# VectorE's order in the second half of an attention-and-MLP pass: the reciprocal behind the first two maxima, the normalisation behind the sixth, the first gate behind the seventh

## The chip, the core and the metric

The kernel runs on one core of one Trainium2 chip. Its time is the device time of one execution in microseconds (us), lower is better; the number that counts is the median of several executions. The core has TensorE (PE in the rows, its weight loads PEld), VectorE (DVE), ScalarE (ACT), GpSimd (POOL) and SyncE (SP, which here only issues DMAs). Each engine works through its own list of instructions in the order in which the program gives them, and waits for the others by semaphores.

## What is computed

The input is 16 sequences of 256 tokens with 288 channels, and a conditioning vector for each. A rotation comes first (a 64-dimensional subspace of the channels is rotated by a matrix exponential made from the conditioning), and then three transformer layers of the same form, of which this is the core:

```
ada = silu(c) @ W_ada + b_ada              # six rows of 288: shifts, scales, gates
h = modulate(layernorm(x), shift_a, scale_a)
q, k, v = split(h @ W_qkv + b_qkv)         # 16 heads of 18
attn = softmax(q @ k.T * 18 ** -0.5)       # over 256 keys
x = x + gate_a * ((attn @ v) @ W_proj + b_proj)
h = modulate(layernorm(x), shift_f, scale_f)
x = x + gate_f * (gelu(h @ W_fc1 + b_fc1) @ W_fc2 + b_fc2)
```

## The kernel before

**Stages.** `prepare` computes the rotation and the conditioning rows; the rest, about nine tenths of the time, is `layers`. There one *pass* works on one sequence of one layer; 3 layers of 16 sequences are 48 passes, numbered `it = l * B + b`. Matrix products are done with a value split in a high and a low part (`split`), so that most operands exist twice: the high part is written by ScalarE, and GpSimd subtracts it from the full value (`low`) for the low part.

**A pass is a software pipeline over three sequences.** `half_step(l, b)` is written once for each engine, and each engine's version says what that engine does in pass `it`: the softmax and weighted values of sequence `it`, the output projection and MLP of `it - 1`, and the queries, keys, scores and maxima of `it + 1` (the norm of `it + 2` too). `whole_run` calls `prologue`, then the passes (the ones with b from 2 to 13 in a loop, b = 0, 1, 14 and 15 written out, since weights are converted in them), then `epilogue`. Nothing but the written order and the semaphores decides what stands behind what.

**TensorE's second half of a pass** (`half_step` of the tensor block): `up(m, 0)` to `up(m, 4)` are the first MLP product of the sequence before, with `score_units(it + 1, 0)` ahead of `up(m, 3)`. Then come `attention_transposes(it + 2)`, `score_units(it + 1, 2)`, `down(m, 0, 0)`, `down(m, 0, 1)`, `score_units(it + 1, 4)`, `down(m, 0, 2)`, `down(m, 1, 0)`, `score_units(it + 1, 6)`, `down(m, 1, 1)`, `down(m, 1, 2)`. A call of `score_units(it, u)` makes the raw scores of the head pairs u and u + 1 in the two PSUM tiles `scores0` and `scores1` (L1840); from u = 2 on it waits until VectorE has read both tiles (`s_max`). The next pass begins with `projection(it, 0)` (L1754 with `w_out`, `o_att`), which waits for both halves of `o_att`'s low part (`s_o_lo`) and for the first gate (`s_down_gated`), then `maxima_transposes`, `projection(it, 1)`, `qk_tiles`, and later `mlp_transposes` (L1770), which waits for VectorE's second `qk_low` and for `x_hat`.

**VectorE's second half of a pass**: `inverse(it)` takes the reciprocal of the softmax sums (L2093; 128 x 32 elements that arrive by a DMA, `s_sum`). `unit_max(it + 1, u)`, eight times, reduces the scores of one head pair to maxima (L2088). `normalise(it)` multiplies the attention output `o_full` by the inverse sums in two halves (L2100), once these have been spread over partitions by four DMAs (`s_inv_ld`). `gate_down(it - 1, t)` multiplies the second MLP product by its gate (L2136), for the two halves t of the tokens; it frees the PSUM tile that the projection of the next pass writes. The next pass begins with `gate_projection` (L2108), `mlp_norm` (L2026, L2031), `qk_low` (L2064) and `x_hats` (L2041).

**ScalarE** issues the DMAs around the sums from its own queue, between its other work: `gather_sums` (L1628), `load_sums` (L1633), and then, between the five `gelu` calls (L1661, L1662), `store_inverse` (L1642, waits for the reciprocal) behind `gelu(2)`, and `spread_inverse` (L1648) behind `gelu(3)` and `gelu(4)`. Behind them come `high_o` (L1638, the high part of `o_att`, waits for `normalise`) and the six evictions of `attention_modulate(it + 2)` (L1574).

**GpSimd** does the low parts. Its list around the end of a pass is

```
for half in range(2): low(o_att[1][:, half, :], ...)   # s_o_lo, L1395
add_mlp(it - 1, 0)        # x_out, waits for gate_down(it - 1, 0), L1523
attention_low(it + 2)     # h_att, two instructions, L1395
add_mlp(it - 1, 1)        # x_out, waits for gate_down(it - 1, 1)
# next pass
add_attention(it)         # x_one, two halves, L1486: waits for gate_projection
inverse_deviation(1, it)  # the norm's rstd, L1390, L1392
```

VectorE's `mlp_norm` waits for `x_one`, its `x_hats` for `rstd`.

Of the kernel before, what the change touches and what calls it, by code (L numbers as in the profile page):

```python
# [998 lines left out]
def layers(nc, dram, keep):  # L999
# [3 lines left out]
    with ExitStack() as ctx:  # L1003
# [262 lines left out]
        def neighbours(l, b):  # L1266

            start = isinstance(l, int) and isinstance(b, int) and l == 0 and b == 0
            final = isinstance(l, int) and isinstance(b, int) and l == L - 1
            return not start, not (final and b >= B - 1), not (final and b >= B - 2)  # L1270
# [741 lines left out]
        def _(dve):  # L2012
# [20 lines left out]
            def x_hats(order, it, x_tile, done):  # L2033
                dve.wait_ge(s_var[order], 2 * it + 2)
                dve.wait_ge(s_rstd[order], it + 1)
                for t in range(2):

                    for out, part in ((x_hat[:, t, 0:C], x_tile[:, t, :]),
                                      (x_hat[:, t, C:MOD_WIDTH].rearrange("p (n c) -> p n c", n=2),
                                       x_tile[:, t, 2 * P:C].unsqueeze(1).to_broadcast([P, 2, C - 2 * P]))):  # L2040
                        nc.vector.tensor_scalar(out, part, mean_var[:, t, 0:1], rstd[:, 1, t:t + 1],  # L2041
                                                ALU.subtract, ALU.mult).then_inc(done, 1)
# [16 lines left out]
            def qk_low(it, n):  # L2059
                dve.wait_ge(s_qk_hi, QK_USES * it + n + 1)  # L2060
                tiles = slice(2 * n, min(2 * n + 2, QK_TILES))
                rows = qk_rows_of(2 * n)
                width = (tiles.stop - tiles.start) * T
                tt(qk[1][0:rows, tiles, :].rearrange("p a t -> p (a t)"), qk_bank[n][0:rows, 0:width],  # L2064
                   qk[0][0:rows, tiles, :].rearrange("p a t -> p (a t)").bitcast(F32), ALU.subtract)\
                    .then_inc(s_qk_lo, 1)
# [24 lines left out]
            def inverse(it):  # L2091
                dve.wait_ge(s_sum, 16 * it + 16)
                nc.vector.reciprocal(inv_few[:, :], sums[:, :]).then_inc(s_inv, 1)  # L2093
# [8 lines left out]
            def gate_projection(it):  # L2102
                dve.wait_ge(s_gate_a, 16 * it + 16)
                for t in range(2):
                    dve.wait_ge(s_proj, 2 * it + t + 1 + PRE)

                    dve.wait_ge(s_x_out, 2 * it - 1 + t + PRE2)
                    tt(gated[:, t, :], token_bank[t][:, 0:C], gate_a[:, :], ALU.mult).then_inc(s_proj_gated, 1)  # L2108

            def mlp_norm(it):  # L2110
                norm(1, it, x_one, lambda t: dve.wait_ge(s_x_one, 2 * it + t + 1 + PRE), s_xhat_m)
# [35 lines left out]
            def half_step(l, b):  # L2147
                it = l * B + b
                before, after, after_next = neighbours(l, b)
                if before:  # L2150
                    gate_projection(it - 1)
                    mlp_norm(it - 1)
                if after:
                    qk_low(it + 1, 0)
                if before:

                    dve.wait_ge(s_tr_a, TRS * (it + 2 if after else it + 1))
                    x_hats(1, it - 1, x_one, s_xhat_m)
                if after:
                    qk_low(it + 1, 1)  # L2160
                    qk_low(it + 1, 2)
                if before:
                    mlp_modulate(it - 1, it + 2 if after else it + 1)
                    mlp_high(it - 1)
                if after_next:
                    attention_norm(it + 2)
                if after_next:

                    dve.wait_ge(s_tr_a, TRS * (it + 2))
                    dve.wait_ge(s_tr_m, TRS * it + PRE)  # L2170
                    x_hats(0, it + 2, x_in, s_xhat_a)
                if at(b, 1):
                    convert_weights(l, OF["w_down"], "down")
                if at(b, B - 2) and after_next:

                    dve.wait_ge(s_qk_ps, QK_USES * (it + 2))
                    convert_weights(l + 1, OF["w_in"], "qk")
                if at(b, B - 1) and after:

                    dve.wait_ge(s_v_ps, 2 * it + 2 + PRE)  # L2180
                    convert_weights(l + 1, OF["w_in"], "v")
                inverse(it)
                if at(b, 1):
                    convert_weights(l, OF["b_down"], "down")
                for u in range(8):
                    if u == 4:
                        normalise(it)
                    if u == 6 and before:
                        gate_down(it - 1, 0)
                    if after:  # L2190
                        unit_max(it + 1, u)
                if before:
                    gate_down(it - 1, 1)
# [135 lines left out]
```

## Time and profile before

| | us |
|---|---|
| median of 3 runs (lowest, highest) | 2189.09 (2180.36, 2191.14) |
| the profiled execution, its own time | 2181.43 |
| span of the instructions in it | 2179.7 |
| TensorE busy (share of the span) | 1946.7 (89%) |
| VectorE busy | 1202.7 (55%) |
| ScalarE busy | 1172.5 (54%) |
| GpSimd busy | 1163.0 (53%) |

A pass lasts some 39 us. The profile has one line for each engine and group of instructions, a list of waits (who was idle until whom) and a timeline of one stretch. All times inside the program are counted from the start of the span. In the timeline a line merges neighbours of one kind: start, length, engine, line of the program, what is written from what, count, and in brackets the idle time before it with the instruction that ended it. The letters PEclk stand for the clock that TensorE was granted, as a share of full speed. The passage that the prediction follows is pass 19 (layer 1, b = 3), which begins its second half at 1006 us and whose reciprocal starts at 1012.99.

### The profile page before, as it was taken

What the parts mean: (1) busy time and instruction counts of PE and PEld (TensorE: products, weight loads), DVE (VectorE), ACT (ScalarE), POOL (GpSimd) and SP (SyncE); (2) the same over time, 40 slices, a digit from 0 to 9 for tenths busy, and PEclk for the clock granted to TensorE, in tenths of its full rate; (3) what the DMA queues carried; (4) which work ended last, traced back from release to release, by engine and by line L of the source; (5) the groups of instructions that cost most, each with busy time, mean ns of one, the idle gap of its engine ahead of it and who ended that gap; (6) DMA issues with size and microseconds to landing.
All of it is one profiled execution on the core that took longest, in us unless ns stands there. A gap on an engine that the chain in (4) does not pass through costs nothing. (4 is left out here: it accounts for less than half of the span.)

```text
span 2179.7 us, 51741 instructions
## 1 busy us (share of the span) xinstructions
PE 1946.7 (89%) x17367; PEld 1652.0 (76%) x17367; DVE 1202.7 (55%) x2735; ACT 1172.5 (54%) x2026; POOL 1163.0 (53%) x1511
## 2 busy tenths in 40 slices
PE   5785689999999898889999999999799999999987
PEld 2554578888888787678888888787678888888876
DVE  6883555455455575555465464574565455554641
ACT  3333455656556555555656556555555556555553
POOL 1003555655555555755655655656655656555543
PEclk9896799999999999999999999999999999999998
DMA  6432433323323333433323323233323323333220
GB/s 181 118 119 86 145 94 87 98 75 101 94 68 106 86 86 97 145 93 83 101 76 94 101 81 100 79 89 108 123 76 92 101 70 106 85 90 94 75 77 25
DMA packets 113198, 207.41 MB, mean 95 GB/s; under 512 B 46213, under 2 KB 62723, under 8 KB 112047
## 3 DMA queue, kind: packets, MB, share of 16 engines
q1 hardware_dynamic: 62766, 127.30, 20.8%
q0 software_dynamic: 25296, 49.71, 8.0%
q10 hardware_dynamic: 25040, 29.18, 4.8%
q8 instruction: 53, 0.87, 0.2%
q14 instruction: 43, 0.34, 0.0%
HBM read 99.51 MB, written 20.82 MB: 55 GB/s over the span
## 5 line engine op out<-in xcount | busy, mean ns | idle before, releaser
L2088 DVE TENSOR_REDUCE maxima<-scores 128x4 f32<-128x1024 f32 x384 | 449.5, 1213 | 91.0 <-PE scores L1840 90.9
L1903 PE MATMUL mlp_ps<-h_mlp,w_up 128*128 128x256 f32 (+1 forms) x3024 | 421.8, 291 | 29.6 <-ACT hidden L1662 26.0
L1903 PEld LDWEIGHTS mlp_ps<-h_mlp,w_up 128*128 128x128 f32 (+1 forms) x3024 | 377.3, 191 | 72.3 <-ACT hidden L1662 34.6
L1614 ACT ACTIVATE probs<-scores 128x1024 f32<-128x1024 f32 x384 | 372.4, 1023 | 82.7 <-PE scores L1864 79.4
L1754 PE MATMUL mlp_ps<-w_down,hidden 128*128 128x288 f32 x2592 | 395.5, 306 | 0.0
L1754 PEld LDWEIGHTS mlp_ps<-w_down,hidden 128*128 128x128 f32 x2592 | 365.6, 195 | 12.2
L1395 POOL TENSOR_TENSOR hidden<-g_full,hidden 128x512 fp32r<-128x512 f32 (+1 forms) x240 | 278.9, 1174 | 153.6 <-ACT hidden L1662 152.6
L1283 POOL DMA_DIRECT2D k_stack<-qk x576 | 295.5, 528 | 30.1 <-issue 18.8
L2093 DVE RECIPROCAL inv_few<-sums 128x32 f32<-128x32 f32 x48 | 16.9, 353 | 452.9 <-DMA sums<-sum_scratch 452.9
L1840 PE MATMUL scores<-k_stack,q_stack 54*128 54x256 f32 x1536 | 149.0, 315 | 95.4 <-DVE maxima L2088 73.1
L1661 ACT ACTIVATE g_full<-mlp_ps 128x512 f32<-128x512 f32 (+1 forms) x240 | 133.3, 555 | 162.1 <-issue 56.4
L1395 POOL TENSOR_TENSOR o_att<-o_full,o_att 128x512 fp32r<-128x512 f32 x96 | 121.8, 1290 | 173.5 <-ACT o_att L1638 173.5
L1840 PEld LDWEIGHTS scores<-k_stack,q_stack 54*128 54x128 f32 x1536 | 109.0, 195 | 134.4 <-DVE maxima L2088 82.7
L1395 POOL TENSOR_TENSOR h_mlp<-h_full,h_mlp 128x512 fp32r<-128x512 f32 x48 | 72.3, 1507 | 246.4 <-DVE h_mlp L2054 246.2
L1878 PE MATMUL pv_ps<-probs,v_sb 128*32 128x256 f32 x3072 | 200.9, 391 | 0.8 <-ACT probs L1614 0.8
L1754 PE MATMUL mlp_ps<-w_out,o_att 128*128 128x288 f32 x1152 | 172.7, 300 | 1.7 <-issue 1.7
L1754 PEld LDWEIGHTS mlp_ps<-w_out,o_att 128*128 128x128 f32 x1152 | 158.9, 191 | 3.1 <-issue 2.1
L1864 PE MATMUL scores<-q_stack,k_stack 55*128 55x256 f32 x1536 | 146.1, 310 | 4.5 <-ACT probs L1614 3.1
L1604 ACT ACTIVATE neg_max<-att_ps 16x256 fp32r<-16x256 f32 x48 | 18.0, 374 | 234.5 <-PE att_ps L1850 234.5
L1864 PEld LDWEIGHTS scores<-q_stack,k_stack 55*128 55x128 f32 x1536 | 106.4, 190 | 49.2 <-ACT probs L1614 29.5
L1811 PE MATMUL att_ps<-h_att,w_in 128*108 128x256 f32 (+3 forms) x1008 | 137.4, 284 | 5.8 <-POOL h_att L1395 5.1
L1878 PEld LDWEIGHTS pv_ps<-probs,v_sb 128*32 128x32 f32 x3072 | 86.0, 111 | 67.0 <-issue 12.9
(230 smaller groups left out, 2921.1 us busy)
## 6 DMA issues: line engine op xcount, KB each, us to landing
q_stack<-qk SPq DMA_DIRECT2D x288, 90.0 KB
k_stack<-qk POOLq DMA_DIRECT2D x288, 90.0 KB, 3.2
inv_sum<-inv_scratch ACTq DMA_DIRECT2D x192, 128.0 KB, 2.6
k_stack<-qk POOLq DMA_DIRECT2D x288, 54.0 KB, 3.5
x_mid<-out_x SPq DMA_DIRECT2D x48, 288.0 KB, 4.2
out_x<-x_out SPq DMA_DIRECT2D x48, 288.0 KB, 3.1
x_in<-out_x SPq DMA_DIRECT2D x47, 288.0 KB, 4.0
q_stack<-qk SPq DMA_DIRECT2D x144, 54.0 KB
```

The source lines that it names most:

```text
L1283: engine.dma_start(stack[first:first + HD, units, :].bitcast(F32), qk[part][row:row + HD, src, :].bitcast(F32)).then_inc(signal, 16)
L1395: tt(out, full, high.bitcast(F32), ALU.subtract).then_inc(signal, 1)
L1604: evict(neg_max[:, :], att_ps[0:H, 0:T], ACT.Copy, scale=-1.0).then_inc(s_neg, 1)
L1614: evict(probs[:, u % 4, :, :, :], scores[u % 2][:, :, :, :], ACT.Exp, scale=SCALE)\
L1661: evict(g_full[:, n % 2, 0:width], bank[:, 0:width], ACT.Gelu_apprx_tanh).then_inc(s_gelu, 1)
L1754: last = mm(out, a(left), c(weights[w]), start=start and n == 0, stop=stop and n == total - 1)
L1811: last = mm(qk_bank[n][0:cols.stop - cols.start, (m % 2) * T:(m % 2 + 1) * T], w[:, cols], h, start=count == 0, stop=count == 6)
L1840: last = mm(scores[v % 2][:, par, qt, :], q_stack[r, v, qt * P:(qt + 1) * P], k_stack[r, v, :], start=True, stop=True, tile_position=(R * ...
L1864: last = mm(scores[v % 2][:, par, kt, :], k_stack[r, v, kt * P:(kt + 1) * P], q_stack[r, v, :], start=True, stop=True, tile_position=(R * ...
L1878: last = mm(pv_ps[32 * i:32 * i + 32, (g % 2) * T:(g % 2 + 1) * T], v_sb[:, kt, 4 * g + i, :], probs[:, u % 4, i % 2, kt, :], start=kt == ...
L1903: last = mm(up_bank[n % 2][:, (m % 2) * T:(m % 2 + 1) * T], w[:, m * P:(m + 1) * P], h, start=count == 0, stop=count == 6)
L2088: nc.vector.tensor_reduce(out=maxima[:, :, :, u].rearrange("p q r -> p r q"), in_=scores[u % 2][:, :, :, :], axis=AX.X, op=ALU.max).then_i ...
```

## The change

The three steps `inverse`, `normalise` and the first `gate_down` are called at other places between the eight `unit_max`. Nothing else is touched: the instructions, their waits and the lists of all other engines stay as they were.

```diff
-                inverse(it)
                 if at(b, 1):
                     convert_weights(l, OF["b_down"], "down")
                 for u in range(8):
-                    if u == 4:
+
+                    if u == 2:
+                        inverse(it)
+                    if u == 6:
                         normalise(it)
-                    if u == 6 and before:
+                    if u == 7 and before:
                         gate_down(it - 1, 0)
                     if after:
                         unit_max(it + 1, u)
```

VectorE in the looped passes, first around the reciprocal (L2093), behind the `x_hat` of the sequence two ahead. In the list `x2`, `x4` count merged instructions; ISA rows are waits, REGISTER_ALU rows compute the value waited for.

```order
 L2041 TENSOR_SCALAR x_hat<-x_in,mean_var,rstd 128x64
+L2084 ISA
+L2088 TENSOR_REDUCE maxima<-scores 128x2x2
+L2084 REGISTER_ALU
+L2088 TENSOR_REDUCE maxima<-scores 128x2x2
 L2092 ISA
 L2093 RECIPROCAL inv_few<-sums 128x32
-L2084 ISA
+L2084 REGISTER_ALU
 L2088 TENSOR_REDUCE maxima<-scores 128x2x2
```

The first two maxima now stand ahead of the reciprocal and of its wait for the sums (L2092).

VectorE, same passes, the end of the list up to the second gate, before:

```order
866 L2096 ISA
867 L2100 TENSOR_TENSOR o_full<-o_full,inv_sum 128x512 x2
868 L2084 REGISTER_ALU
869 L2088 TENSOR_REDUCE maxima<-scores 128x2x2
870 L2084 REGISTER_ALU
871 L2088 TENSOR_REDUCE maxima<-scores 128x2x2
872 L2136 TENSOR_TENSOR gated<-mlp_ps,gate_f 128x288
873 L2084 REGISTER_ALU
874 L2088 TENSOR_REDUCE maxima<-scores 128x2x2
875 L2084 REGISTER_ALU
876 L2088 TENSOR_REDUCE maxima<-scores 128x2x2
877 L2136 TENSOR_TENSOR gated<-mlp_ps,gate_f 128x288
```

and in the changed kernel:

```order
867 L2084 REGISTER_ALU
868 L2088 TENSOR_REDUCE maxima<-scores 128x2x2
869 L2084 REGISTER_ALU
870 L2088 TENSOR_REDUCE maxima<-scores 128x2x2
871 L2096 ISA
872 L2100 TENSOR_TENSOR o_full<-o_full,inv_sum 128x512 x2
873 L2084 REGISTER_ALU
874 L2088 TENSOR_REDUCE maxima<-scores 128x2x2
875 L2136 TENSOR_TENSOR gated<-mlp_ps,gate_f 128x288
876 L2084 REGISTER_ALU
877 L2088 TENSOR_REDUCE maxima<-scores 128x2x2
878 L2136 TENSOR_TENSOR gated<-mlp_ps,gate_f 128x288
```

The fifth and sixth maxima have moved ahead of the normalisation (L2100) and its wait (L2096), and one more maximum stands ahead of the first gate (L2136).

## Rows read from the trace of the kernel before

**Rows 1.** The page, part 1: busy time, share of the span, instructions.

```profile
PE 1946.7 (89%) x17367; PEld 1652.0 (76%) x17367; DVE 1202.7 (55%) x2735; ACT 1172.5 (54%) x2026; POOL 1163.0 (53%) x1511
```

**Rows 2.** The waits: who for whom, us in total, times, longest.

```profile
DVE inv_few L2093 <- DMA sums<-sum_scratch: 452.9, 48, 14.3
...
PE scores L1840 <- DVE maxima L2088: 73.1, 47, 5.2
```

**Rows 3.** Timeline of TensorE, 1009 to 1036 us (pass 19).

```profile
1010.30 0.73 PE L1840 MATMUL scores<-k_stack,q_stack 54*128 54x256 f32 x8 [0.56 <-DMA k_stack<-qk]
...
1014.01 0.38 PE L1770 MATMUL pv_ps<-ident,x_hat 128*96 128x128 f32 x2
1015.61 0.74 PE L1840 MATMUL scores<-k_stack,q_stack 54*128 54x256 f32 x8 [1.22 <-DVE maxima L2088]
1016.52 0.40 PE L1912 MATMUL mlp_ps<-b_down,ones_l 128*128 128x288 f32 x1 [0.18 <-ACT hidden L1662]
...
1019.23 0.74 PE L1840 MATMUL scores<-k_stack,q_stack 54*128 54x256 f32 x8
...
1025.77 1.75 PE L1754 MATMUL mlp_ps<-w_out,o_att 128*128 128x288 f32 x12
```

**Rows 4.** Timeline of VectorE, 960 to 1060 us (pass 19's part).

```profile
1012.99 0.35 DVE L2093 RECIPROCAL inv_few<-sums 128x32 f32<-128x32 f32 x1 [9.74 <-DMA sums<-sum_scratch]
...
1016.16 2.36 DVE L2088 TENSOR_REDUCE maxima<-scores 128x4 f32<-128x1024 f32 x2 [0.61 <-PE scores L1840]
1018.85 1.30 DVE L2100 TENSOR_TENSOR o_full<-o_full,inv_sum 128x512 f32<-128x512 f32 x2 [0.33 <-DMA inv_sum<-inv_scratch]
1020.06 2.35 DVE L2088 TENSOR_REDUCE maxima<-scores 128x4 f32<-128x1024 f32 x2
1022.32 0.45 DVE L2136 TENSOR_TENSOR gated<-mlp_ps,gate_f 128x288 f32<-128x288 f32 x1
...
1030.75 0.46 DVE L2026 BATCH_NORM_STATS2 stats<-x_one 128x6 f32<-128x288 f32 x1 [0.56 <-POOL x_one L1486]
```

**Rows 5.** Timeline of all engines, 1006 to 1060 us: ScalarE's.

```profile
1019.57 1.24 ACT L1638 ACTIVATE o_att<-o_full 128x512 fp32r<-128x512 f32 x2 [1.40 <-DVE o_full L2100]
...
1022.96 0.56 ACT L1574 ACTIVATE h_att<-pv_ps,mods 96x256 fp32r<-96x256 f32 x1
```

**Rows 6.** The same timeline, GpSimd's.

```profile
1020.28 2.54 POOL L1395 TENSOR_TENSOR o_att<-o_full,o_att 128x512 fp32r<-128x512 f32 x2 [3.00 <-ACT o_att L1638]
...
1022.93 0.80 POOL L1523 TENSOR_TENSOR x_out<-x_one,gated 128x288 f32<-128x288 f32 x1
...
1023.68 2.10 POOL L1395 TENSOR_TENSOR h_att<-h_full,h_att 128x512 fp32r<-128x512 f32 x2
...
1026.51 0.80 POOL L1523 TENSOR_TENSOR x_out<-x_one,gated 128x288 f32<-128x288 f32 x1 [0.73 <-DVE gated L2136]
...
1029.90 0.81 POOL L1486 TENSOR_TENSOR x_one<-x_mid,gated 128x288 f32<-128x288 f32 x1 [0.92 <-DVE gated L2108]
```

**Rows 7.** Timeline of TensorE's weight loads, 1009 to 1036 us.

```profile
1034.97 0.63 PEld L1770 LDWEIGHTS mlp_ps<-ident,x_hat 128*128 128x128 f32 x6 [0.19 <-DVE qk L2064]
```

**Rows 8.** Timeline of TensorE, 835 to 846 us (pass 15, b = 15).

```profile
838.92 0.74 PE L1840 MATMUL scores<-k_stack,q_stack 54*128 54x256 f32 x8
...
843.62 0.40 PE L1912 MATMUL mlp_ps<-b_down,ones_l 128*128 128x288 f32 x1
```

**Rows 9.** Timeline of VectorE, 836 to 843 us (pass 15).

```profile
839.14 0.35 DVE L2093 RECIPROCAL inv_few<-sums 128x32 f32<-128x32 f32 x1 [12.85 <-DMA sums<-sum_scratch]
```

**Rows 10.** Timeline of all engines, 930 to 938 us (pass 17, b = 1).

```profile
931.64 0.35 DVE L2093 RECIPROCAL inv_few<-sums 128x32 f32<-128x32 f32 x1 [7.37 <-DMA sums<-sum_scratch]
...
936.83 0.40 PE L1912 MATMUL mlp_ps<-b_down,ones_l 128*128 128x288 f32 x1
```

**Rows 11.** Windows, reciprocal to reciprocal, of passes 19 and 6: length, busy times, PEclk, DMA share, GB/s.

```profile
1012.99:1051.65 38.66, 37.27 (x337) 32.09 (x336) 21.38 (x40) 23.01 (x38) 22.54 (x31) 1.00 0.34 92
473.03:513.33 40.30, 38.42 (x336) 33.33 (x335) 21.47 (x41) 23.01 (x38) 22.64 (x31) 0.96 0.32 88
```

## The prediction, made before the changed kernel ran

> **What bounds the kernel now.** I read the page first [rows 1]: TensorE is busy for 89% of the span, every other engine for about half of it. So only what makes TensorE wait, or takes a wait from it, changes the time. The waits come second [rows 2]: the longest of all, 452.9 us in 48 passes, is VectorE's for the sums ahead of the reciprocal, and it costs VectorE nothing it needs; the one that the change is about is TensorE's for the maxima, 73.1 us in 47 waits. Third, the timeline of one pass. In pass 19 TensorE is through with the transposes of `x_hat` at 1014.01 + 0.38 = 1014.39, waits 1.22 us for the first two maxima, makes the scores from 1015.61 to 1016.35, waits once more, 0.18 us, for ScalarE's last gelu, and begins the second MLP product at 1016.52 [rows 3]. The maxima are late because VectorE has them behind the reciprocal, whose sums land only at 1012.99 [rows 4], although their scores were begun at 1010.30 [rows 3]. In 36 of the 39 passes with b from 2 to 14 these distances are the same (the second scores start 2.61 to 2.62 us behind the reciprocal). From 1016.52 on TensorE has no gap above 0.2 us up to 1035; `mlp_transposes` at 1034.97 then wait 0.19 us for VectorE [rows 7]. That is the bound in one sentence: sums, reciprocal, the rest of the gelus, and from there TensorE itself, with its neighbours just in time.
>
> **The change, part by part**, in pass 19 and against its own clock times.
>
> *Two maxima ahead of the reciprocal.* The first maximum of a pair starts 1016.16 - 1015.61 = 0.55 us behind the start of its scores, and two take 2.36 us [rows 3, 4]. With scores at 1010.30 they run from 1010.85 to 1013.21, and the reciprocal, which overlaps the last one by some 0.08 us, starts at 1013.13 instead of 1012.99. It is late where the scores lead it by less than 2.83 us. Over the 39 passes the lead is 2.3 to 3.7 us with a median of 3.05; in those that fall short the shortfalls add up to 1.6 us in all, which I take as the price.
>
> *What TensorE gets.* Its second scores can start at 1014.39 instead of 1015.61, so the wait of 1.22 us goes. What is late next is ScalarE: store of the reciprocal, `gelu(3)`, the first two spreading DMAs and `gelu(4)` stand in one queue behind the reciprocal, and the second MLP product starts 1016.52 - 1012.99 = 3.53 us behind it, today with 0.18 us of wait for that gelu [rows 3, 4]. The reciprocal comes no earlier, so the product starts at 1016.52 as before, only that TensorE now waits 1.4 us ahead of it in one piece. Gain: 0. The third and fourth maxima get earlier, and nobody waits for them: the next scores stand behind 18 products and start at 1019.23 either way [rows 3].
>
> Here a rule of the Trainium skill speaks the other way. Its page "Perfetto Trace Analysis", section "Optimization Strategy", says to look for the gaps of the engine that bounds the kernel, find the semaphore behind each, and make that dependency come sooner, which is what this edit does. By it alone the time would fall by all of the 73.1 us; by the row of the next wait it falls by nothing. The rule is silent on a second wait right behind the first.
>
> *The normalisation behind the sixth maximum.* Today it starts at 1018.85, as soon as its DMAs land [rows 4]. In the new order it stands behind the maxima 5 and 6, whose scores start at 1019.23 [rows 3]: first maximum at 1019.23 + 0.55 = 1019.78, and the instruction behind a pair starts 1022.32 - 1020.06 = 2.26 us after the pair [rows 4], so 1022.04. That is 3.19 us later. Behind it hang, with their durations unchanged: ScalarE's high parts (1019.57), GpSimd's low parts (from 1020.28 for 2.54 us, end 1022.82, that is 3.97 us behind the normalisation's start) and ScalarE's six evictions for the sequence after next (end 1023.52) [rows 4 to 6]. The low parts now end at 1022.04 + 3.97 = 1026.01. The projection waits for them, and starts today at 1025.77 [rows 3]: it had 2.95 us to spare and is asked for 3.19. With about 0.1 us for the semaphore (an estimate, from the 0.05 to 0.2 us between end and start in these rows) it starts 0.35 us late. In return the seventh and eighth scores no longer wait for a VectorE held up by the normalisation (some 0.1 us), which the wait for the low parts swallows.
>
> *What is queued behind on GpSimd.* This is the larger term. Today GpSimd has room after the low parts: `x_out` 1022.93, `h_att` from 1023.68 for 2.10 us, then a gap of 0.73 us, `x_out` 1026.51, a gap, `x_one`, a gap of 0.92 us, `x_one` from 1029.90 to 1030.71 [rows 6]. Shifted, the same list runs without a gap: first `x_out` 1026.12, `h_att` 0.75 us later at 1026.87 (ScalarE's evictions end at 1023.52 + 3.19 = 1026.71, just in time), end 1028.97, second `x_out` 1029.07, then the two `x_one` at 0.75 us each, 1029.82 and 1030.57, end 1030.57 + 0.81 = 1031.38. That is 0.67 us later than 1030.71. VectorE's statistics start 0.04 us behind this end today [rows 4]; on them hang `rstd`, `x_hat` and, in VectorE's list behind `x_hat`, the second `qk_low`, for which TensorE's transposes wait [rows 7]. So TensorE, already 0.35 us late, waits 0.3 us more there and is 0.67 us late in all. Nothing behind it takes this back: TensorE is the bound from there to the weighted values, and the sums of the next reciprocal hang on those. So a pass becomes 0.67 us longer.
>
> *The first gate behind the seventh maximum.* VectorE's list: normalisation 1022.04 to 1023.34, seventh maximum, gate at about 1024.4, end 1024.85, eighth maximum, second gate at 1025.97 as today. The first gate moves by about 2.1 us; its readers are the projection, which now starts at 1026.1, and the first `x_out`, at 1026.12. Cost 0; without the late low parts it would have had 0.9 us to spare. SP's queue gets its next gate load and store behind other waits of the next pass: 0.
>
> *The passes written out.* b = 15, two times with a successor: scores come late there, at 838.92, so the reciprocal moves from 839.14 to 838.92 + 2.83 = 841.75; the product starts 3.53 us behind it, at 845.3, today at 843.62 [rows 8, 9]: +1.65 each, with the 0.67 together +4.6. b = 1, three times: today the conversion of `b_down` stands between reciprocal and maxima, and the product starts at 936.83; with the maxima made earlier it starts 3.53 us behind the reciprocal, 931.64 + 3.53 = 935.17 [rows 10]. I take -1.66 twice and -0.8 in the first layer, with the 0.67 -2.1. b = 0: there the normalisation waits long for its DMAs and holds back maxima 5 and 6; that goes, but GpSimd's queue then sets the pace: -0.5 each, between 0 and -2.4. Pass 0: +0.9. Pass 46 lacks `h_att` on GpSimd: +0.35.
>
> **The sum**: 38 x 0.67 = 25.5; reciprocals 1.6; 4.6 - 2.1 - 1.0 + 0.9 + 0.35 = 2.8; together +29.9 us. Against the profiled execution's own time, 2181.4, this is 2211. The median of the three runs lies 7.7 us above that execution and the lowest below it, so I add half of the distance: **2215 us**. Bounds of the one unknown, the handover: 0.05 us instead of 0.1 makes 0.6 a pass (+27), a further 0.2 us somewhere in GpSimd's list, which has no gap left, 0.87 (+37).
>
> **Rivals.**
> *Faster.* The wait for the maxima was the true limit and the gelus would come in time, or 1.4 us in one piece is worth more than two waits. It decides at the start of the second product: only if it comes earlier than 3.53 us behind the reciprocal. The most it can give is 73.1 us (2181 - 73 = 2108). Against it stands the 0.18 us that TensorE waits there for ScalarE today [rows 3]. 4%.
> *No change.* The normalisation had slack, as the 2.95 us say, and `x_one` is taken in time because GpSimd's list runs closer than its rows. Then only the written-out passes and the reciprocals count, 1.6 + 1.0: 2184 to 2192. It decides whether `x_one` ends later than 1030.71 on pass 19's clock. 10%.
> *Slower through the clock.* Pass 6 is 40.30 us long, pass 19 38.66; in pass 6 the granted clock averages 0.96, in 19 it is 1.00 [rows 11]: that is some 3 us (0.04 x 40.30 / 0.5) at the lower of the two levels, 1.2 instead of 2.4 GHz, and they follow the idle time ahead of the second product. In 8 of the 39 passes this happens, for about 1.5 us each. The new order joins the idle pieces and adds two short ones; if every pass fell, 30 x 1.5 = 45 us would be added: 2260. The idle sum ahead of the product is the same (1.4 us), so I expect the number of such passes to stay near 8, within 5: 7.5 us either way. The Trainium skill ("TensorE: Matmul & The Clock Gate", section "HAM oscillation — how this bites in real kernels") tells of kernels that fall back to the lower level at each wait; here most passes wait and do not fall. 6% for a fall in most passes.
>
> **How the numbers follow.** The forecast, with its mechanism and 20 to 45 us more, has 80%. The range reaches from 2200 (0.45 us a pass against the profiled execution) to 2236 (0.87 a pass, against the highest run, and a few more slow stretches). 0.5%, 11 us, is what a measurement of this kernel can tell from no change. Faster by more than that 5%, within it 10%, slower 85%.
>
> **What the profile of the changed kernel would show.** TensorE's wait for L2088 nearly gone, and in its place one of about 1.4 us a pass for ScalarE's `hidden` ahead of L1912. The product 3.53 us behind the reciprocal, as now. The normalisation 2.8 us behind the start of the third pair of scores. A new wait of TensorE for GpSimd's `o_att` ahead of the projection, about 0.3 to 0.5 us, and one of about as much for VectorE's `qk` ahead of L1770. GpSimd without a gap from `o_att` to the second `x_one`. Passes of 39.3 us instead of 38.7. The prediction is wrong if the product starts earlier behind the reciprocal, if the projection waits for nobody and `x_one` ends no later against it, or if the slow stretches of the clock change by more than five.

## The result, and the profile after

| | before | after |
|---|---|---|
| median, us (lowest to highest) | 2185.86 (2180.36 to 2191.14) | 2224.24 (2220.32 to 2230.86) |
| ratio, 95% interval | | 1.0179 (1.0141 to 1.0217) |
| span of the profiled execution, us | 2179.7 | 2223.3 |
| granted clock of TensorE over the span | 0.956 | 0.945 |
| second MLP product behind the reciprocal, us | 3.52 | 3.51 |
| normalisation behind the reciprocal | 5.99 | 9.05 |
| GpSimd's low parts of `o_att` end behind it | 9.97 | 13.01 |
| projection starts behind it | 12.78 | 13.15 |
| second `x_one` ends behind it | 17.73 | 18.44 |
| `mlp_transposes` start behind it | 21.98 | 22.49 |
| projection to projection, undisturbed passes | 38.81 | 39.26 |

Slower, as forecast, and inside the range. The rows from the third on are medians over the passes with b = 3 to 13 in which TensorE's clock did not fall and GpSimd's DMA issue was not held up: 24 passes before, 19 after ("undisturbed passes" below; the six places in a pass, each as its distance from the reciprocal, are called landmarks).

The page of the changed kernel, parts 1 and 2:

```profile
PE 1973.9 (89%) x17367; PEld 1673.3 (75%) x17367; DVE 1201.9 (54%) x2735; ACT 1171.9 (53%) x2026; POOL 1159.8 (52%) x1511
...
PEclk9896799999999998999999999998999999999998
```

Against [rows 1], TensorE is busy 27 us longer with the same 17367 products. Nothing was added to its work, so some of it ran slower; this is the first sign of the part that the prediction had at zero. The waits (who for whom, us in total, times, longest):

```profile
PE mlp_ps L1912 <- ACT hidden L1662: 72.6, 43, 3.1
...
PE mlp_ps L1754 <- POOL o_att L1395: 14.9, 41, 6.2
...
PE scores L1840 <- DVE maxima L2088: 11.2, 7, 2.0
```

The wait for the maxima, 73.1 us before [rows 2], is down to 11.2, and 72.6 us stand in the next line of TensorE's list, the wait for ScalarE's last gelu. The wait for `o_att` is new. The timeline of TensorE in pass 19, whose reciprocal now starts at 1031.61:

```profile
1032.48 0.38 PE L1770 MATMUL pv_ps<-ident,x_hat 128*96 128x128 f32 x2
1032.79 0.73 PE L1840 MATMUL scores<-k_stack,q_stack 54*128 54x256 f32 x8
1035.14 0.40 PE L1912 MATMUL mlp_ps<-b_down,ones_l 128*128 128x288 f32 x1 [1.62 <-ACT hidden L1662]
...
1037.87 0.74 PE L1840 MATMUL scores<-k_stack,q_stack 54*128 54x256 f32 x8
...
1044.79 1.85 PE L1754 MATMUL mlp_ps<-w_out,o_att 128*128 128x288 f32 x12 [0.23 <-POOL o_att L1395]
```

These answer to [rows 3]: the scores follow the transposes at once, the product is still 1035.14 - 1031.61 = 3.53 us behind the reciprocal, and the projection waits for GpSimd at 13.18 us, where it started at 12.78. VectorE and GpSimd in the same pass:

```profile
1038.42 2.36 DVE L2088 TENSOR_REDUCE maxima<-scores 128x4 f32<-128x1024 f32 x2 [2.73 <-PE scores L1840]
1040.69 1.28 DVE L2100 TENSOR_TENSOR o_full<-o_full,inv_sum 128x512 f32<-128x512 f32 x2
...
1052.26 1.21 DVE L2041 TENSOR_SCALAR x_hat<-x_one,mean_var,rstd 128x288 f32<-128x288 f32 x4 [0.52 <-POOL rstd L1392]
1053.39 0.68 DVE L2064 TENSOR_TENSOR qk<-mlp_ps,qk 126x512 fp32r<-126x512 f32 x1
```

```profile
1042.11 2.54 POOL L1395 TENSOR_TENSOR o_att<-o_full,o_att 128x512 fp32r<-128x512 f32 x2 [6.21 <-ACT o_att L1638]
1044.62 0.80 POOL L1523 TENSOR_TENSOR x_out<-x_one,gated 128x288 f32<-128x288 f32 x1
1045.49 2.09 POOL L1395 TENSOR_TENSOR h_att<-h_full,h_att 128x512 fp32r<-128x512 f32 x2
1047.74 0.81 POOL L1523 TENSOR_TENSOR x_out<-x_one,gated 128x288 f32<-128x288 f32 x1 [0.16 <-POOL h_att L1395]
1048.51 1.56 POOL L1486 TENSOR_TENSOR x_one<-x_mid,gated 128x288 f32<-128x288 f32 x2
```

The normalisation follows the maxima without a gap, and GpSimd goes from `o_att` to the second `x_one` with one gap of 0.16 us, where it had three [rows 6].

The other part is the clock. Windows of the changed kernel, reciprocal to reciprocal, of pass 19 and of passes 37 to 40: length; busy time of PE, PEld, DVE, ACT, POOL; PEclk, DMA share, GB/s:

```profile
1031.61:1070.95 39.34, 37.23 (x333) 31.78 (x333) 21.34 (x41) 23.00 (x38) 21.95 (x31) 1.00 0.33 90
1773.61:1814.81 41.20, 39.38 (x343) 34.25 (x342) 21.53 (x42) 22.99 (x38) 23.72 (x31) 0.96 0.30 86
1814.81:1855.36 40.55, 38.01 (x330) 32.81 (x329) 21.50 (x41) 23.00 (x38) 22.03 (x31) 0.96 0.32 87
1855.36:1896.59 41.23, 38.87 (x337) 33.46 (x336) 21.52 (x41) 22.99 (x38) 22.87 (x31) 0.96 0.30 86
1896.59:1937.53 40.94, 38.83 (x336) 33.59 (x335) 21.50 (x41) 23.00 (x38) 22.86 (x31) 0.96 0.31 87
```

A pass in which TensorE falls to the lower level (1.2 GHz, half speed) behind the idle time ahead of the product is some 1.5 us longer. Of the 39 passes with b from 2 to 14 this happened in 11 before and in 18 after, and after it happened in rows: 6 to 9, 37 to 42. (The prediction counted 8 before; the other three are passes 12, 28 and 43, where GpSimd's issue of a DMA is held up, by 5.2 us in pass 12 before, and the product comes 5.2 to 9.0 us behind the reciprocal in every kernel that left ScalarE's queue alone.) Over the whole span TensorE had the lower level for 2 x (1 - 0.956) x 2179.7 = 192 us before and 2 x (1 - 0.945) x 2223.3 = 245 us after. If TensorE bounds the kernel in that time, half of the difference, 26 us, is lost. That is an upper estimate: the falls counted here are seven more, with one each in passes 15 and 31 nine more, and at 1.5 us each that is 13.5 us. The other part is the longer undisturbed pass, 39.26 - 38.81 = 0.45 us, 21 us in 47 passes.

Where the 43.6 us by which the span grew really lie can be summed from reciprocal to reciprocal. The 36 passes with b from 2 to 13 are 26.9 us longer in sum: 36 x 0.45 = 16.2 us and five more falls, 7.5 us, give 23.7 of it. Passes 14 and 15 together are 6.4 us longer, passes 30 and 31 8.5 us (a fall in each of the four is new; the rest is below, with the passes written out). Everything else, the time ahead of the first reciprocal and behind the last included, comes to 1.8 us.

### The profile page after: what moved, and what is told of

Its sections match the earlier page's. It is cut to its first block and busy times, and to the rows that moved or that the text cites. A ratio compares the mean times of both kernels' runs of the same rounds, so it can differ in the third digit from the quotient of the medians.

```text
span 2223.3 us, 51741 instructions
## 1 busy us (share of the span) xinstructions
PE 1973.9 (89%) x17367; PEld 1673.3 (75%) x17367; DVE 1201.9 (54%) x2735; ACT 1171.9 (53%) x2026; POOL 1159.8 (52%) x1511
## 5 line engine op out<-in xcount | busy, mean ns | idle before, releaser
L2088 DVE TENSOR_REDUCE maxima<-scores 128x4 f32<-128x1024 f32 x384 | 455.9, 1219 | 584.1 <-PE scores L1840 583.9
L1903 PE MATMUL mlp_ps<-h_mlp,w_up 128*128 128x256 f32 (+1 forms) x3024 | 421.9, 292 | 25.5 <-ACT hidden L1662 22.0
L1754 PE MATMUL mlp_ps<-w_down,hidden 128*128 128x288 f32 x2592 | 413.9, 315 | 0.0
L1754 PEld LDWEIGHTS mlp_ps<-w_down,hidden 128*128 128x128 f32 x2592 | 383.4, 204 | 12.6 <-issue 1.0
L1638 ACT ACTIVATE o_att<-o_full 128x512 fp32r<-128x512 f32 x96 | 59.2, 632 | 265.9 <-DVE o_full L2100 265.9
L1754 PE MATMUL mlp_ps<-w_out,o_att 128*128 128x288 f32 x1152 | 177.8, 305 | 16.5 <-POOL o_att L1395 14.9
L1840 PE MATMUL scores<-k_stack,q_stack 54*128 54x256 f32 x1536 | 150.3, 317 | 30.5 <-DMA q_stack<-qk 13.5
L1811 PEld LDWEIGHTS att_ps<-h_att,w_in 128*108 128x108 f32 (+3 forms) x1008 | 128.6, 180 | 10.0 <-issue 6.6
```

The source lines that it names most:

```text
L1638: evict(o_att[0][:, half, :], o_full[:, half, :], ACT.Copy).then_inc(s_o_hi, 1)
L1754: last = mm(out, a(left), c(weights[w]), start=start and n == 0, stop=stop and n == total - 1)
L1811: last = mm(qk_bank[n][0:cols.stop - cols.start, (m % 2) * T:(m % 2 + 1) * T], w[:, cols], h, start=count == 0, stop=count == 6)
L1840: last = mm(scores[v % 2][:, par, qt, :], q_stack[r, v, qt * P:(qt + 1) * P], k_stack[r, v, :], start=True, stop=True, tile_position=(R * ...
L1903: last = mm(up_bank[n % 2][:, (m % 2) * T:(m % 2 + 1) * T], w[:, m * P:(m + 1) * P], h, start=count == 0, stop=count == 6)
L2088: nc.vector.tensor_reduce(out=maxima[:, :, :, u].rearrange("p q r -> p r q"), in_=scores[u % 2][:, :, :, :], axis=AX.X, op=ALU.max).then_i ...
```

## The experiments

**One part at a time.** The first question was which of the three moves costs, and whether the clock has a cause of its own. Two theories were put against each other: A, the late normalisation, and B, the joined idle time that lets the clock fall.

Only the reciprocal moved:

```diff
-                inverse(it)
                 for u in range(8):
+                    if u == 2:
+                        inverse(it)
                     if u == 4:
                         normalise(it)
```

> Only the reciprocal is moved (behind the first two maxima); normalisation behind the fourth, first gate behind the sixth, as before. Theory A (the loss is the late normalisation): TensorE's wait for L2088 ahead of the second scores falls from 1.2 to about 0, its wait for ScalarE ahead of the second MLP product grows from 0.2 to 1.4 us, the product stays 3.5 us behind the reciprocal; undisturbed passes 38.8 us as before, ratio 0.998 to 1.003. Theory B (the idle pieces joined into one make TensorE's clock fall more often): time at the lower clock grows from 196 us towards the 246 us of the changed kernel, ratio 1.010 with unchanged undisturbed passes.

Measured: 2210.29 us, ratio 1.0120 (1.0079 to 1.0161). Undisturbed passes 38.90 us (38.81 before), the product 3.52, the projection 12.79, the transposes 21.99 us behind the reciprocal: all within 0.1 us of before. The clock fell in 19 of the 39 passes, six in a row from pass 20 to 25. The windows of the pass ahead of that row and of the first two in it:

```profile
1022.03:1060.62 38.59, 37.39 (x338) 32.37 (x339) 21.45 (x41) 23.04 (x38) 23.80 (x31) 1.00 0.34 91
1060.62:1101.10 40.48, 38.70 (x338) 33.70 (x337) 21.61 (x41) 23.04 (x38) 22.90 (x31) 0.96 0.31 88
1101.10:1142.52 41.42, 38.85 (x339) 33.85 (x338) 21.63 (x41) 23.04 (x38) 23.60 (x31) 0.96 0.31 86
```

So theory A, which had this edit at 0.998 to 1.003, is wrong for it, and B is right in the main: the move that was to take a wait away costs 1.2% by itself. Eight more falls in the 39 passes and one in pass 31 are some 13.5 of the 23.8 us by which its span is longer than before.

Only the normalisation moved:

```diff
-                    if u == 4:
+                    if u == 6:
                         normalise(it)
                     if u == 6 and before:
                         gate_down(it - 1, 0)
```

> Only the normalisation is moved (behind the sixth maximum); reciprocal first, gate behind the sixth. Theory A: the projection waits for GpSimd about 0.3 us, the transposes for VectorE, undisturbed passes 39.25 us as in the changed kernel, ratio 1.010 (+21 us, 47 passes of 0.45) or more if the clock falls oftener too. Theory B: the idle pieces ahead of the product are as before, so the time at the lower clock stays near 196 us; if all of the loss was the clock, ratio 1.000.

Measured: 2208.73 us, ratio 1.0113 (1.0062 to 1.0165). Undisturbed passes 39.27 us, low parts 13.03, projection 13.16, `x_one` 18.45, transposes 22.50; the clock fell in 9 passes. TensorE in its pass 19, whose reciprocal starts at 1025.95 (the clock fell in this one, so all behind it is 1.5 us later):

```profile
1028.56 0.74 PE L1840 MATMUL scores<-k_stack,q_stack 54*128 54x256 f32 x8 [1.38 <-DVE maxima L2088]
...
1040.64 1.85 PE L1754 MATMUL mlp_ps<-w_out,o_att 128*128 128x288 f32 x12 [0.23 <-POOL o_att L1395]
```

The wait for the maxima ahead of the second scores is there as before, the wait for `o_att` is the new one. This is theory A alone, 47 x 0.46 = 22 us, 1.0% of the time. Both theories hold, each for its own part of the change.

Only the first gate moved:

```diff
-                    if u == 6 and before:
+                    if u == 7 and before:
                         gate_down(it - 1, 0)
```

> Only the first gate is moved (behind the seventh maximum). Theory A: it is read by the projection and the first x_out, both with time to spare: undisturbed passes 38.8 us, ratio 0.998 to 1.002. Rival C (the late gate holds the PSUM tile or GpSimd's list): up to +0.5 us a pass, ratio 1.01.

Measured: 2190.16 us, ratio 1.0031 (1.0004 to 1.0058). The landmarks of undisturbed passes are those of before to 0.01 us (product 3.52, projection 12.79, transposes 21.98), the passes 38.83 us. The clock fell in 14 passes; 0.3% is what is left, and nothing in an undisturbed pass shows it. Rival C is out: it had up to 0.5 us in each pass. Whether the 0.3% is more than the clock's own spread stays open.

The normalisation one maximum earlier, in the changed kernel:

```diff
-                    if u == 6:
+                    if u == 5:
                         normalise(it)
```

> The changed kernel with the normalisation one maximum earlier, behind the fifth. Theory A with its sum: normalisation 7.9 us behind the reciprocal instead of 9.06, low parts end 11.9 (projection wants them at 12.65), GpSimd's second x_one ends 17.3, before the 17.72 that gated1 allows: both waits go completely, undisturbed passes 38.8 us, ratio near 1.000 to 1.003. If the loss grew in proportion to the delay instead, half of it would stay (39.0 us, 1.005 or more). Theory B: the idle piece ahead of the product is still joined, time at the lower clock near 246 us, ratio 1.010.

Measured: 2246.03 us, ratio 1.0291 (1.0247 to 1.0334), undisturbed passes 39.65 us, and the clock fell in 17. Both sums failed, and the reason is a wait that I had left out. The timeline of TensorE in pass 4, reciprocal at 408.95:

```profile
415.18 0.74 PE L1840 MATMUL scores<-k_stack,q_stack 54*128 54x256 f32 x8
...
419.35 0.74 PE L1840 MATMUL scores<-k_stack,q_stack 54*128 54x256 f32 x8 [0.73 <-DVE maxima L2088]
```

The seventh scores wait for the sixth maximum, and the normalisation now stands between the fifth and the sixth. The low parts do end in time (11.86 us), but the scores start at 10.39 instead of 9.59 us and the projection at 13.55. Behind the sixth maximum, where the change puts it, the normalisation is at least out of the way of those scores. Put between the two maxima of one pair, the normalisation is paid for by these scores and by GpSimd's list.

**Is it the clock?** The idle time ahead of the product was filled with work that nobody needs. In `score_units(it, u)` the scores of the second pair are made three times over into the same tiles, and signalled after the last:

```diff
                 for v in (u, u + 1):
-                    for qt in range(2):
+                    for qt in (0, 1) * (3 if u == 2 else 1):
```

With the reciprocal's move alone:

> The kernel with only the reciprocal moved, and TensorE makes its second scores three times over instead of once (same tiles, same values, signalled after the last), so that the 1.35 us ahead of the second MLP product are filled with work that nobody needs. Clock theory (the loss of recip_only is passes in which TensorE falls to the lower clock behind that idle time): falls at 3.4 to 4.6 us behind the reciprocal go from 16 in 33 regular passes to 0 to 3, the product stays at 3.5 us, undisturbed passes 38.9 us, ratio 0.99 to 1.000. Rival (the loss comes from b = 15 and the other written-out passes): regular passes unchanged, ratio stays at 1.012.

Measured: 2181.37 us, ratio 0.9983 (0.9965 to 1.0001). The clock fell in 3 of 39 passes (12, 28 and 43), and the product stayed at 3.51 us. TensorE in an undisturbed pass, reciprocal at 1050.95, and the windows of the three passes from there:

```profile
1051.90 1.70 PE L1840 MATMUL scores<-k_stack,q_stack 54*128 54x256 f32 x24
1054.48 0.40 PE L1912 MATMUL mlp_ps<-b_down,ones_l 128*128 128x288 f32 x1 [0.88 <-ACT hidden L1662]
```

```profile
1050.95:1089.94 38.99, 37.66 (x350) 32.66 (x350) 21.44 (x40) 23.01 (x38) 23.27 (x31) 1.00 0.33 91
1089.94:1129.25 39.31, 38.26 (x356) 33.28 (x354) 21.52 (x41) 23.11 (x38) 23.28 (x31) 1.00 0.33 91
1129.25:1168.04 38.79, 37.63 (x350) 32.62 (x349) 21.48 (x40) 23.01 (x38) 22.99 (x30) 1.00 0.32 90
```

16 more products a pass (24 instead of 8 for the second pair) cost nothing and bring the time back to that of the kernel before. The order of the work is the same, with less idle time in front of the product. The clock is not all of the 1.2%, though: the filling also removes falls that the kernel before has, eight of its 11, which at 1.5 us should win 12 us against it, and the medians differ by 5.6. One piece of the rest can be seen. Passes 14 and 15 together are still 1.4 us longer than before, passes 30 and 31 1.6 us, by the late reciprocal that the prediction had there.

In the changed kernel:

> The changed kernel with the same filling. Clock theory: what is left of the loss is the normalisation's place, 0.45 us a pass: undisturbed passes 39.3 us, hardly any falls in regular passes, ratio 1.000 to 1.006 instead of 1.018. Rival: ratio stays at 1.018.

Measured: 2206.08 us, ratio 1.0096 (1.0062 to 1.0130), above the 1.000 to 1.006 that was expected; undisturbed passes 39.18 us, the clock fell in 4 passes, granted clock 0.956. Without most of the falls 0.8 of the 1.8% are gone. Of the 20.4 us by which the span is longer than before, 6.6 lie in the 36 passes with b from 2 to 13 (16 us for the normalisation, less seven falls), 7.9 in passes 14, 15, 30 and 31, and the other 5.9 outside of both; the last is open.

**What bounds the second product.** The prediction said: ScalarE's gelus, which stand in one queue behind the store of the reciprocal. ScalarE in pass 19 of the changed kernel shows them (ACTq are the DMAs that it issues):

```profile
1032.00 0.35 ACTq L1642 DMA_DIRECT2D inv_scratch<-inv_few  x1
1032.52 0.60 ACT L1661 ACTIVATE g_full<-mlp_ps 128x512 f32<-128x512 f32 x1 [2.08 <-PE mlp_ps L1903]
...
1033.45 0.80 ACTq L1648 DMA_DIRECT2D inv_sum<-inv_scratch  x2
1034.43 0.38 ACT L1661 ACTIVATE g_full<-mlp_ps 128x256 f32<-128x256 f32 x1 [0.83 <-issue]
```

So the store was moved behind `gelu(3)`, and the spreading DMAs behind `gelu(4)`:

```diff
                         gelu(it - 1, n)
-                        if n == 2:
-                            store_inverse(it)
                         if n == 3:
-                            spread_inverse(it, (0, 1))
-                    spread_inverse(it, (2, 3))
+                            store_inverse(it)
+                    spread_inverse(it, (0, 1, 2, 3))
```

In the changed kernel:

> The changed kernel; ScalarE issues the store of the reciprocal behind gelu(3) instead of behind gelu(2) and all four spreading DMAs behind gelu(4), so that its gelus no longer stand behind the reciprocal. Theory A (reciprocal, then two gelus in ScalarE's queue, bound the second product): product 2.2 us behind the reciprocal instead of 3.5, undisturbed passes 37.9 us, less idle time and so fewer falls of the clock, ratio 0.975 to 0.985. Rival (the product is bound by the gelus' own work or by GpSimd's low parts): product stays at 3.5, ratio 1.018.

Measured: 2134.05 us, ratio 0.9758 (0.9726 to 0.9789): 2.4% faster than the kernel before and 4.1% faster than the changed one. The timeline of TensorE in pass 20, reciprocal at 1035.36 (two lines of the program less, so L1838 and L1910 are the scores and the product):

```profile
1036.48 0.38 PE L1768 MATMUL pv_ps<-ident,x_hat 128*96 128x128 f32 x2
1036.79 0.74 PE L1838 MATMUL scores<-k_stack,q_stack 54*128 54x256 f32 x8
1037.45 0.40 PE L1910 MATMUL mlp_ps<-b_down,ones_l 128*128 128x288 f32 x1
...
1047.09 1.85 PE L1752 MATMUL mlp_ps<-w_out,o_att 128*128 128x288 f32 x12 [0.23 <-POOL o_att L1395]
```

Transposes, scores and product follow each other without a gap; the product is 1.9 us behind the reciprocal in the median instead of 3.5. Undisturbed passes are 37.89 us, the clock fell in 3 passes, and the projection still waits for GpSimd, since the normalisation stands where the change put it. Store and spreading DMAs were moved together, so their shares are not told apart.

The same edit in the kernel before:

> The same edit of ScalarE's queue in the kernel before, where the maxima stand behind the reciprocal. Theory A: the second scores still start 2.61 us behind the reciprocal and the product right behind them at 3.4 to 3.5, so nothing is won: ratio 0.995 to 1.003. If it is won here too, the maxima's place did not matter.

Measured: 2185.23 us, ratio 0.9996 (0.9973 to 1.0019). Undisturbed passes 38.59, product at 3.28 us, the clock fell in 7 passes. As expected nothing is won: there the maxima, behind the reciprocal, hold the second scores.

With only the reciprocal moved:

> ScalarE's later store together with the reciprocal's move alone (normalisation behind the fourth maximum, gate behind the sixth). If the whole change is what pays in after_late_store, this one loses most of it: the spreading DMAs land about 6.3 us behind the reciprocal, the normalisation waits for them and holds up the fifth maximum, whose scores are there at 4.8, so the seventh scores start at about 9.6 instead of 8.1: undisturbed passes near 38.8, ratio 0.99 to 1.00. If the normalisation's place does not matter here: passes of 37.5 us and a ratio of 0.97.

Measured: 2225.7 us, ratio 1.0159 (1.0110 to 1.0208), undisturbed passes 38.94 us, about as expected, the time above the 0.99 to 1.00 that was expected. VectorE and TensorE in pass 20, reciprocal at 1085.53:

```profile
1091.52 1.29 DVE L2098 TENSOR_TENSOR o_full<-o_full,inv_sum 128x512 f32<-128x512 f32 x2 [1.87 <-DMA inv_sum<-inv_scratch]
1092.73 2.35 DVE L2086 TENSOR_REDUCE maxima<-scores 128x4 f32<-128x1024 f32 x2
```

```profile
1095.13 0.74 PE L1838 MATMUL scores<-k_stack,q_stack 54*128 54x256 f32 x8 [1.56 <-DVE maxima L2086]
```

The product comes at 1.86 us, but the normalisation waits for its DMAs, the fifth and sixth maxima stand behind it, and the seventh scores wait 1.56 us: the gain is handed back in full. The clock then falls behind this wait instead (in 16 of the 39 passes at 9.8 to 12.9 us behind the reciprocal; granted clock 0.939 over the span), which is what the expectation lacked. Against `after_late_store`, which differs from this kernel in the places of the normalisation and the first gate, 4% are lost: here the normalisation's late place is what pays, the same place that costs 1% while the store is early.

**GpSimd's list.** `x_out` was computed on 32 of 288 channels only (in the changed kernel; the other channels of the result are left at zero):

```diff
-                tt(x_out[:, t, :], x_one[:, t, :], gated[:, t, :], ALU.add)
+                tt(x_out[:, t, 0:32], x_one[:, t, 0:32], gated[:, t, 0:32], ALU.add)
```

> The changed kernel, with GpSimd's two x_out additions done on 32 of the 288 channels (the rest of the result is left at zero), which takes some 1.2 us out of its list around the end of a pass. If the full list is what makes the second x_one late: x_one ends near 17.7 us behind the reciprocal instead of 18.44, the transposes start 22.3 instead of 22.5 (the projection's own lateness of 0.38 us stays), undisturbed passes 39.1 instead of 39.26 us. Rival (the transposes are late only through the projection): x_one earlier, transposes unchanged at 22.5.

One execution took 2236.16 us; the clock fell in 23 passes. The 13 undisturbed ones are 39.38 us long, against the 39.1 expected. `x_one` ends at 18.21, not 17.7, and the transposes start at 22.46, not 22.3 (22.49 in the changed kernel). The list of GpSimd in pass 20:

```profile
1094.11 0.24 POOL L1524 TENSOR_TENSOR x_out<-x_one,gated 128x32 f32<-128x32 f32 x1
1094.99 2.11 POOL L1396 TENSOR_TENSOR h_att<-h_full,h_att 128x512 fp32r<-128x512 f32 x2 [0.64 <-ACT h_att L1575]
```

What the shorter `x_out` gave, GpSimd then waited for ScalarE's evictions, which hang on the same normalisation. And `x_one` 0.23 us earlier moved the transposes by only 0.03. The second `qk_low`, for which they wait, needs `x_hat` and ScalarE's high part of `qk`. In the undisturbed passes `x_hat` ends at 21.13 us before, 21.84 in the changed kernel and 21.54 here; ScalarE's part ends at 21.20, 21.67 and 21.68, and `qk_low` starts at 21.23, 21.75 and 21.72. So with `x_one` out of the way it stands on ScalarE, whose part is 0.47 us later than before because the projection and the products behind it are. The expectation was wrong on both counts, and its rival, that the transposes are late only through the projection, is nearly right.

## The prediction, point by point

**What bounds the kernel**: right. The product stays 3.51 to 3.53 us behind the reciprocal in every kernel that left ScalarE's queue alone, and goes to 1.9 when that queue is changed and the maxima come first (3.28 when it is changed alone).

**Two maxima ahead of the reciprocal, gain 0, price 1.6 us over all**: the gain of 0 is right, and the wait reappeared one line further as forecast (73.1 us there, 72.6 here). The price is where the prediction failed: the move costs 1.2% alone. The step at fault is the sentence that the idle sum ahead of the product stays the same, so that the falls of the clock stay near 8, within 5. The falls went from 11 to 18, or in the prediction's count from 8 to 15; a change of more than five was one of its own signs of being wrong. The idle sum nearly stayed: in pass 19 1.22 + 0.18 = 1.40 us before and 1.62 after, in the median 1.38 and 1.56. Whether the added falls come from its being in one piece, without scores in between, or from the 0.18 us more, no run separates. The 1.6 us that it gave for late reciprocals is also a wrong sum: by its own rule (a lead of less than 2.83 us) the shortfalls of the 39 passes add up to 3.0.

**The normalisation, and the projection 0.35 us late**: right to a few hundredths. Forecast from pass 19's rows, as distances from the reciprocal: normalisation 9.05, low parts 13.02, projection 13.13; measured there 9.08, 13.04, 13.18.

**GpSimd's queue, and 0.67 us a pass**: the mechanism is there, the size is not. `x_one` ends at 18.45 us in pass 19, forecast 18.39. But its 0.7 us of lateness arrive at the transposes as 0.51 us and at the next projection as 0.45. The term that was mis-sized is the slack between `x_hat` and the second `qk_low`, which I took as none. In the kernel before, `x_hat` ends 0.10 us ahead of that `qk_low`, which waited for ScalarE:

```profile
1032.90 1.22 DVE L2041 TENSOR_SCALAR x_hat<-x_one,mean_var,rstd 128x288 f32<-128x288 f32 x4 [0.31 <-POOL rstd L1392]
1034.22 0.69 DVE L2064 TENSOR_TENSOR qk<-mlp_ps,qk 126x512 fp32r<-126x512 f32 x1
```

In the changed kernel (1052.26 and 1053.39 above) it follows `x_hat` at once. The extra 0.3 us of wait that the prediction had for `qk` ahead of L1770 is not there either: the weight loads wait for it 13.2 us in total before and 14.2 after. The forecast of 0.67 x 38 = 25.5 us would be 0.45 x 38 = 17.1 with the measured size. GpSimd's list is also not the larger term, as I had it: of the 0.51 us, ScalarE's high part of `qk`, which hangs on the projection's 0.37 and the products behind it, carries 0.47.

**The first gate, 0**: right for the landmarks, 0.3% left open.

**The passes written out**: the product of pass 17 (b = 1) is at 3.53 us behind the reciprocal instead of 5.18, as forecast, but in pass 1 it went from 4.34 to 5.20 and in pass 33 from 5.12 only to 4.20, where 3.53 was forecast. ScalarE's last gelu is held there by other things: in pass 1 ScalarE is idle for 2.50 us until the store of the reciprocal has landed, for which its spreading DMAs wait, and in pass 33 for 1.57 us until GpSimd has its low part. In passes 15 and 31 the product is at 3.53, behind a reciprocal that now follows the maxima by construction (scores 2.94 us ahead of it instead of 0.22 and 0.03). The 1.65 us forecast for each of them is borne out by `recip_fill`, where the clock hardly plays a part: passes 14 and 15 together are 1.4 us longer than before, 30 and 31 1.6. In the changed kernel they are 6.4 and 8.5 us longer, where the forecast had 3.0 (1.65 and twice 0.67) and four new falls make 3.0 more in each two; the rest of the second is open.

**The sum**: +29.9 us against 43.6 in the profiled executions, 2215 against a median of 2224. The direction held because of the normalisation. That the number lies inside the range, 2200 to 2236, is partly luck: the clock, which was put at nothing, is worth 13.5 to 26 us of the 43.6, the 0.67 was some 8 us too large, and the two errors have opposite signs.

**The rival "slower through the clock"**, 6% for most passes: it came halfway, in 18 of 39 passes where 11 had it before. The Trainium skill ("TensorE: Matmul & The Clock Gate", section "HAM oscillation — how this bites in real kernels") describes a kernel that falls at each wait and advises to order the loop so that TensorE stays busy; the fill experiments agree with the advice (1.0120 to 0.9983). Its example has TensorE waiting longer than it works, while here TensorE fell in about every second pass with some 1.6 us of wait ahead of the product in a pass of 39.

**The rule of the Trainium skill** ("Perfetto Trace Analysis", section "Optimization Strategy") that speaks for the edit, to make the dependency behind a gap come sooner, gave 2108 us by itself. The runs disagree for the edit alone (2210 and 2224 us), and agree in direction once the second wait behind the first is taken away too: 2134.

## What to carry to other kernels

A wait that is removed from the bounding engine is worth only the distance to the next wait in that engine's list; read that one before costing the first, and change both together. A step that is moved out of one engine's way moves everything behind it on three others. The starts of what hangs on it directly could be forecast from one timeline to a few hundredths of a microsecond; three steps further on, where two engines' results meet, the slack was missed by 0.2 us, because only one of the two had been read. When two short waits of TensorE become one longer one, look at the granted clock pass by pass: here the sum of idle time, nearly unchanged, did not tell what the clock would do.

## What was not expected of the hardware

TensorE fell to the lower level behind a single idle stretch of about 1.6 us in a pass of 39 us in which it was otherwise busy. One execution of each kernel was profiled, and by the form of the idle time their counts fall into groups: 17 to 23 of 39 passes where it is one stretch of 1.6 us (the changed kernel, `recip_only`, `norm_fifth`, `small_xout`), 9 to 14 where it is 1.4 to 1.5 us in two pieces (before, `norm_only`, `gate_only`), 7 where it is 1.2 us in one piece (`before_late_store`), and 3 or 4 where it is 0.6 us (`recip_fill`, `after_fill`) or none (`after_late_store`). The falls came in rows: ordinary passes that fell are 39.8 to 41.4 us long in the kernel before, the changed one and `recip_only`, and six followed one another in `recip_only` (20 to 25), six in the changed kernel (37 to 42), while the same kernels also had six (37 to 42) and five (23 to 27) in a row without any; why they do is open. Filling 1 us of the stretch with products that nobody reads ended the falls in all ordinary passes with the reciprocal's move alone, at no cost. Falls do not explain every difference that the landmarks leave: before and `gate_only`, with the same landmarks to 0.01 us, had 11 and 14 of them, about 4.5 us, and their spans differ by 14.4. And time at the lower level is not always lost: of `gate_only`'s 41 us more of it, 25 lie ahead of the first reciprocal, which comes only 2.1 us later.
